# Moving K and V of the fourth attention into earlier stages, waiting for weights a stage later, and a shared expert with features on partitions

## The chip, the cores and the metric

One Trainium2 chip, one of its cores. The metric is device time in microseconds (us), lower is better. TensorE is PE in the profile, VectorE DVE, ScalarE ACT, GpSimd POOL, and SyncE, which only issues transfers here, SP.

## What is computed

A residual stream x of 4 x 256 tokens with 256 features (1024 tokens in all), and a context of the same size. Eight layers, each `x = x + layer(layernorm(x))`: an attention and a feed-forward layer, four times. The parts that the change touches:

- second attention: softmax attention of q (from x) over the context and over k, v made from x. It reads the context as it is.
- third feed-forward: `relu(x W1.T)**2`, normalised by the root of its mean square, times `W2.T`, with ternary weights.
- fourth attention: 16 heads of 16 features, all 1024 queries over all 1024 keys. `q = x Wq + bq`, `k, v = ctx Wkv + bkv`; q and k are rounded to 127 steps per token and head, v per feature over all tokens; the softmax is rounded to 255 steps per row; then a projection. K and V depend on the context and on weights alone.
- fourth feed-forward: 8 routed experts (512 hidden features, each token goes to two) and one shared expert, `silu(x Wg) * (x Wu) @ Wd` with 1024 hidden features.

## The kernel before, in words

Tokens lie on partitions in 8 tiles of 128 (`X`), or features on partitions in 2 chunks of 128 (`XT`, and `CT` for the context). Each layer is a function of its own with one or two blocks; inside a block every engine runs a list of its own, tied by semaphores, and a block ends when all engines have reached its end, SP among them. So a wait of SP at the end of a block holds all the others.

`layer_norm` (L156) runs ahead of each layer: it normalises x, turns it into `XT`, and meanwhile SP loads the weights of a later stage (L179) and waits for them (L181) before the block can end. It has two options: `ahead` projects the context's tokens on PE before the turning of x (L151, 16 matmuls of 256 columns), `ahead_features` the context's features (L721, 8 matmuls of 512 columns). A float32 matmul shows as two records. Before the change the third attention uses the second option, the fourth attention the first.

`attention_l1` (L1523) is the second attention; its first block projects q, k and v of x (L1556 and on), 8 groups of 2 matmuls with 512 columns, then v.

`ffn_relu2` (L1908) is the third feed-forward layer: 16 units; per unit PE makes two matmuls (L1941), ACT applies relu (L2003), DVE squares (L2018), ACT squares again for the mean, POOL adds it up (L1989). PE's down matmuls (L1946) for the first half lie between units 10 to 13, and those for the second half end the block.

The fourth attention is three functions. `quantise_l3` (L2038): PE projects q and then v (L151, L2074), DVE adds biases, finds the largest of each head, divides and rounds (L2121 to L2144), ACT scales v (L2100 to L2109), PE turns v, SP issues 22 loads of the experts' weights (L2064). `split_store` (L308) splits k into three bfloat16 parts whose sum is k (L334 to L353), turns them and q on PE (L373) and stores both to DRAM (L381). `attention_l3` (L2148) clears the ring buffers, loads 4 heads of q and k, keeps PE busy with 12 matmuls (L2237), and then runs 128 units, 16 heads of 8 query tiles: scores on PE (L2247), maximum on DVE (L2277), exponential to 8 bits on ACT (L2268), a transpose by DMA for every two units (L2209, issued by SP), a cast on POOL (L2224) and the sum over V on PE (L2257). SP also loads the head that comes three later (L2197 q, L2199 k), and an expert's weights in the middle of heads 0 and 1 (L2217). The buffers for the exponentials hold 4 pairs of units.

`moe_silu` (L1327) is the last stage. PE computes the router's logits; DVE chooses experts, PE counts (L1262 to L1268) and DVE places tokens (L1302 to L1323); POOL scatters the rows of x into DRAM, sorted by expert, in 16 indirect transfers (L1367); SP loads them back in 23 blocks (L1385). The order of PE's work is written out by hand. 39 units: 8 of the shared expert (its first 512 hidden features, one token tile each), 23 blocks, 8 of the shared expert (second half). Step n issues:

```
go_up(n); [counts at n == 1]; turn_hidden(n - 1); turn_x of block unit n + 1; go_down(n - 2)
```

`go_up` is 4 matmuls of 512 columns (L1422), `turn_hidden` 4 transposes (L1430), `turn_x` 2 (L1400), `go_down` 4 matmuls of 256 columns (L1444). All downs use one PSUM bank (7), so each waits until DVE has taken the one before (L1514 or L1516). At the end POOL gathers the experts' rows (L1375) and DVE merges them tile by tile (L1496).

## Time and profile before

| | us |
|---|---|
| median of 3 runs (lowest, highest) | 1148.74 (1146.13, 1152.38) |
| the profiled execution, its own time | 1146.27 |
| its span in the profile | 1144.3 |
| mean granted clock of TensorE in it | 0.851 of full speed |

Busy in the profile's span: PE 931.5 us (81%), DVE 620.5 (54%), ACT 539.3 (47%), POOL 254.8 (22%). The page lists the chain of work that ended last as PE for the last 20% of the span, with the lines of `moe_silu`. Busy shares are means over very different stages, and PE counts as busy when it runs at half its clock. So the stages are read one by one, by the times at which their first and last instructions stand in the timeline.

### The profile page before, as it was taken

The page shows a single profiled execution, that of the slowest core. Times are in us where ns is not written, and L with a number is a line of the kernel's source. Part 1 is how long each engine was busy: PE and PEld are TensorE (multiplying, and loading weights), DVE is VectorE, ACT ScalarE, POOL GpSimd, SP SyncE. Part 2 cuts the span into 40 slices and gives each one's busy share as a digit, 9 for nine tenths or more (in the row PEclk, how much of TensorE's full clock was granted, in tenths as well). Part 3 has the DMA queues.
Part 4 walks back from the last instruction along what each step waited for, and adds up shares of the span by engine and source line. Part 5 has one row for each costly group of instructions (what it writes and reads, how often), then busy time and mean ns, then how long its engine had stood idle before and what let it go on. Part 6 is the DMA issues. An engine that isn't in the chain of part 4 may idle for free. (4 is left out here: it accounts for less than half of the span.)

```text
span 1144.3 us, 15734 instructions
## 1 busy us (share of the span) xinstructions
PE 931.5 (81%) x5518; PEld 555.4 (49%) x5544; DVE 620.5 (54%) x1284; ACT 539.3 (47%) x807; POOL 254.8 (22%) x299
## 2 busy tenths in 40 slices
PE   5698887997895458899699547787776699999998
PEld 3244436665584144444367332343344556666665
DVE  4577745545145976354413938999996441111124
ACT  3166673222125745688431247998986122222211
POOL 4011000000000003144231104767675031000023
PEclk9599998998998689999899856555655799999999
DMA  3613301001480005765100936665653311111012
GB/s 124 146 34 77 84 12 42 0 1 51 103 63 28 0 17 177 185 139 81 47 1 1 349 129 120 129 108 112 107 100 70 111 46 60 43 46 46 28 46 84
DMA packets 116494, 90.07 MB, mean 79 GB/s; under 512 B 77829, under 2 KB 104655, under 8 KB 114639
## 3 DMA queue, kind: packets, MB, share of 16 engines
q1 hardware_dynamic: 111570, 81.87, 30.6%
q0 software_dynamic: 1536, 4.20, 1.2%
q10 hardware_dynamic: 3312, 3.02, 0.8%
q8 instruction: 45, 0.74, 0.3%
q14 instruction: 31, 0.25, 0.1%
HBM read 57.66 MB, written 16.38 MB: 65 GB/s over the span
## 5 line engine op out<-in xcount | busy, mean ns | idle before, releaser
L2268 ACT ACTIVATE sb_l_E<-PS,sb_l_NB,sb_L3SQS 128x1024 uint8<-128x1024 f32 x128 | 154.5, 1207 | 23.0 <-DVE sb_l_NB L2280 13.5
L2277 DVE TENSOR_REDUCE sb_l_NM<-PS 128x1 f32<-128x1024 f32 x128 | 155.4, 1214 | 3.8 <-PE PS L2247 3.8
L2247 PE MATMUL PS<-sb_l_K,sb_l_Q 128*128 128x512 bf16 x232 | 115.7, 590 | 43.0 <-ACT sb_l_E L2268 33.9
L2224 POOL CAST sb_l_ET<-sb_l_EP 128x1024 bf16<-128x1024 uint8 x128 | 129.4, 1043 | 64.1 <-DMA sb_l_EP<-sb_l_E 59.6
L682 DVE TENSOR_REDUCE sb_negmax<-PS 128x2 f32<-128x512 f32 x128 | 84.1, 689 | 32.2 <-PE PS L532 31.9
L1468 ACT ACTIVATE sb_hidden<-PS 128x512 f32<-128x512 f32 x39 | 23.3, 598 | 164.5 <-PE PS L1422 164.5
L1503 DVE TENSOR_TENSOR sb_hidden<-sb_hidden,PS 128x512 f32<-128x512 f32 x39 | 26.8, 687 | 125.1 <-ACT sb_hidden L1468 125.1
L2257 PEld LDWEIGHTS PS<-sb_L3VI,sb_l_ET 128*128 128x128 bf16 x1024 | 56.1, 113 | 69.1 <-issue 56.1
L668 ACT ACTIVATE sb_E<-PS 128x1024 f32<-128x1024 f32 x64 | 65.5, 1024 | 42.8 <-PE PS L595 42.8
L1422 PE MATMUL PS<-sb_L3w,sb_block_xT 128*128 x184 | 82.8, 592 | 0.0
L991 ACT ACTIVATE sb_E<-PS 128x1024 f32<-128x1024 f32 x64 | 65.3, 1024 | 24.7 <-PE PS L899 21.0
L532 PE MATMUL PS<-sb_K,sb_Q 96*128 96x256 bf16 x256 | 53.8, 302 | 15.8 <-ACT sb_negmax_T L642 10.3
L915 POOL MEMSET sb_rms_eps<- 128x1 f32 x1 | 0.1, 99 | 275.2 <-POOLq L175 275.2
L1422 PE MATMUL PS<-sb_W,sb_XT 128*128 128x512 f32 x128 | 59.1, 607 | 0.0
L2257 PE MATMUL PS<-sb_L3VI,sb_l_ET 128*128 128x16 bf16 x1024 | 50.8, 179 | 5.7 <-POOL sb_l_ET L2224 5.7
L1193 DVE SCALAR_TENSOR_TENSOR sb_X<-PS,sb_gates,sb_X 128x256 f32<-128x256 f32 x80 | 33.2, 476 | 35.7 <-PE PS L1116 35.7
L1422 PEld LDWEIGHTS PS<-sb_L3w,sb_block_xT 128*128 128x128 f32 x184 | 34.8, 190 | 34.4 <-issue 33.2
L200 PE MATMUL PS<-sb_identf,sb_XN 128*128 128x128 f32 x128 | 24.7, 374 | 32.3 <-DVE sb_XN L235 32.3
L532 PEld LDWEIGHTS PS<-sb_K,sb_Q 96*128 96x128 bf16 x256 | 21.3, 102 | 51.3 <-ACT sb_negmax_T L642 16.5
L595 PE MATMUL PS<-sb_Q,sb_K 128*128 128x512 bf16 x128 | 39.6, 391 | 5.3 <-DMA sb_Q<-sb_negmax_T 5.3
L1444 PE MATMUL PS<-sb_W2E,sb_hidden_T 128*128 x184 | 43.5, 379 | 0.0
L1375 POOL DMA_INDIRECT sb_XN<-ys,sb_slot x8 | 7.6, 952 | 160.0 <-PE PS L1444 157.8
(342 smaller groups left out, 1748.3 us busy)
## 6 DMA issues: line engine op xcount, KB each, us to landing
sb_Q<-q SPq DMA_DIRECT2D x48, 192.0 KB
sb_L3w<-L3w SPq DMA_DIRECT2D x16, 512.0 KB, 9.5
sb_K<-k SPq DMA_DIRECT2D x24, 192.0 KB
sb_W2E<-L3w SPq DMA_DIRECT2D x8, 512.0 KB, 9.4
q<-sb_q_parts SPq DMA_DIRECT2D x12, 256.0 KB, 2.4
xs<-zero_row SPq DMA_DIRECT2D x1, 2944.0 KB, 47.9
sb_block_x<-xs SPq DMA_DIRECT2D x23, 128.0 KB, 2.2
ys<-sb_block_y ACTq DMA_DIRECT2D x23, 128.0 KB, 2.4
```

Of the source, the lines that this page charges most:

```text
L532: ins = pe.matmul(core.PS[:, shared_bank(("max", m)), i * SEQ:(i + 1) * SEQ], Q[0:RK, g % RING, j * TOK + t * P:j * TOK + (t + 1) * P], K[ ...
L595: ins = pe.matmul(core.bank(2 * (s % 2) + n).rearrange("p (j q) -> p j q", q=SEQ), K[0:ROWS, g % RING, keys], q[:, 2 * n:2 * n + 2, b * SE ...
L668: act.activation(E[:, s % ERING].rearrange("p j q -> p (j q)"), core.PS[:, 2 * (s % 2):2 * (s % 2) + 2, :].rearrange("p b n -> p (b n)"), ...
L682: dve.tensor_reduce(NM[:, g, 2 * b:2 * b + 2, j:j + 1], core.bank(shared_bank(("max", m))).rearrange("p (u k) -> p u k", k=SEQ), axis=AX.X ...
L991: act.activation(E[:, s % ERING].rearrange("p j q -> p (j q)"), core.PS[:, 2 * (s % 2):2 * (s % 2) + 2, :].rearrange("p b n -> p (b n)"), ...
L1422: ins = pe.matmul(core.bank(2 * (u % 2) + side), x, w, start=(c == 0), stop=(c == NC - 1))
L1444: ins = pe.matmul(core.PS[:, 7, 0:D], HT[:, u % 2, k, :], w, start=(k == 0), stop=(k == HC - 1))
L2224: return eng.tensor_copy(ET[:, u % CRING], EP[:, u // 2 % TRING, :, :, u % 2])
L2247: ins = pe.matmul(core.bank(2 * (n % SRING) + half), Q[:, h % RING, t * P:(t + 1) * P], K[:, h % RING, half * HALF:(half + 1) * HALF], sta ...
L2257: ins = pe.matmul(core.PS[:, 6 + h % 2, t * HD:(t + 1) * HD], ET[:, u % CRING, k, :], VI[:, k, h * HD:(h + 1) * HD], start=(k == 0), stop= ...
L2268: act.activation(E[:, n // 2 % ERING, :, n % 2], S(n), ACT.Exp, bias=NB[:, n:n + 1], scale=scale_of(h, t), accum_out=ZS[:, n:n + 1]).then_ ...
L2277: dve.tensor_reduce(NM[:, n:n + 1], S(n), axis=AX.X, op=ALU.max, negate=True).then_inc(maxed, 1)
```

## The change

- **Weights.** `layer_norm` no longer waits for the loads that it issues; the next normalisation waits for them before it issues its own (`at_once` keeps the old wait in the first). PE waits there too, when it projects ahead.
- **V of the fourth attention.** Its weights are loaded during the first attention (4 more loads). The third normalisation projects V ahead (`ahead_features`), the first block of the second attention rounds it on ACT and DVE, and two transposes by DMA bring it into place; the clearing of `xs` comes behind them on SP.
- **K.** The normalisation ahead of `ffn_relu2` projects K (`ahead`), the one behind it no longer does. `ffn_relu2` rounds K and splits it on DVE and ACT between its own steps (`key_step`), three DMA transposes of 128 x 2048 turn the parts, and 6 stores bring them to DRAM. The first 10 experts' loads are issued at the start of this function, 6 at its end, in front of its last waits.
- **The fourth attention.** `quantise_l3` and `split_store` are gone. `attention_l3` projects q itself, rounds it in two halves on DVE, turns it on PE in bfloat16 and copies it to SBUF; each head's q is then copied three times from there (3 transfers where there was 1). Two experts' loads go ahead of q's, ten more transfers follow in the middle of heads 0 to 9: 6 of experts and the 4 of the last stage (router, gate, up, down weights) that the last normalisation issued before.
- **The last stage.** A unit of the shared expert is now one chunk of 128 hidden features for 512 tokens: weights are stationary and `XT` moves, so the hidden values come out with features on partitions and need no turning. It has 8 units for the first 512 tokens and 8 for the others. The downs (8 matmuls of 256 columns for each of the 8 token tiles) need all 8 chunks: tiles 0 to 3 are done in steps 9 to 12, between the first blocks, tiles 4 to 7 all after the last unit. The order inside a step is up, turn, shared down, `turn_x`, block down.

```diff
+                if sent_by_now:
+                    sp.wait_ge(core.weights_in, sent_by_now)
                 for dst, src in weights:
-                    sp.dma_start(dst, src).then_inc(loaded, 16)
-                if weights:
-                    sp.wait_ge(loaded, 16 * len(weights))
+                    sp.dma_start(dst, src).then_inc(core.weights_in, 16)
+                if at_once:
+                    sp.wait_ge(core.weights_in, core.weights_sent)
...
+                if sent_by_now and (ahead is not None or ahead_features is not None):
+                    pe.wait_ge(core.weights_in, sent_by_now)
...
-    units = ([("shared", 0, t) for t in range(NT)] + [("block", None, b) for b in range(BLOCKS)]
-             + [("shared", 1, t) for t in range(NT)])
+    SC = 2 * HC
+    units = ([("shared", 0, k) for k in range(SC)] + [("block", None, b) for b in range(BLOCKS)]
+             + [("shared", 1, k) for k in range(SC)])
     NU = len(units)
-    block_unit = lambda b: NT + b
+    block_unit = lambda b: SC + b
+    downs_at = [[] for n in range(NU + 2)]
+    for b in range(BLOCKS):
+        downs_at[block_unit(b) + 2].append(("block", b))
+    for t in range(4):
+        downs_at[SC + 1 + t].insert(0, ("shared", t))
+        downs_at[NU + 1].append(("shared", 4 + t))
+    downs = [d for at in downs_at for d in at]
+    down_count = {d: i + 1 for i, d in enumerate(downs)}
...
-                            x = core.XT[:, c, i * P:(i + 1) * P]
-                            w = WGU[:, side, c, half * HID:(half + 1) * HID]
+                            x = WGU[:, side, c, i * P:(i + 1) * P]
+                            w = core.XT[:, c, half * HALF:(half + 1) * HALF]
...
+            def go_down(kind, i):
+                if down_count[(kind, i)] >= 2:
+                    pe.wait_ge(y_out, down_count[(kind, i)] - 1)
+                if kind == "shared":
+                    pe.wait_ge(hidden, SC if i < 4 else NU)
+                    for k in range(SC):
+                        ins = pe.matmul(core.PS[:, 7, 0:D], HS[:, k, (i % 4) * P:(i % 4 + 1) * P], WD[:, k, :],
+                                        start=(k == 0), stop=(k == SC - 1))
+                else:
+                    pe.wait_ge(h_out, i + 1)
+                    for k in range(HC):
                         w = core.W2E[:, bass.ds(expert[i], 1), k * D:(k + 1) * D].rearrange("p e n -> p (e n)")
-                    ins = pe.matmul(core.PS[:, 7, 0:D], HT[:, u % 2, k, :], w, start=(k == 0), stop=(k == HC - 1))
+                        ins = pe.matmul(core.PS[:, 7, 0:D], HT[:, i % 2, k, :], w, start=(k == 0), stop=(k == HC - 1))
                 ins.then_inc(down, 1)
...
-                if 1 <= n <= NU:
-                    turn_hidden(n - 1)
+                if 1 <= n <= NU and units[n - 1][0] == "block":
+                    turn_hidden(units[n - 1][2])
+                for d in downs_at[n]:
+                    if d[0] == "shared":
+                        go_down(*d)
...
+                        if i >= 4:
                             merge(i)
-
-
-def attention_l1(core, dram, Wq, Wk, Wv, Wo, xs):
+                if n == NU - SC + 7:
+                    for t in range(4):
+                        merge(t)
...
+                for c in range(NC):
+                    sp.wait_ge(v3_rounded, c + 1)
+                    sp.dma_start_transpose(VI[:, :, c * P:(c + 1) * P], VQ[:, c, :]).then_inc(v3_turned, 16)
+                sp.wait_ge(v3_turned, 16 * NC)
...
+            @block.sync
+            def _(sp):
+                for dst, src in experts[:SOON]:
+                    sp.dma_start(dst, src).then_inc(core.experts_in, 16)
+                def turn(i):
+                    sp.wait_ge((k_high, k_middle, k_low)[i], NT // 2)
+                    if i >= 2:
+                        sp.wait_ge(k_stored[i - 2], 16 * NC)
+                    sp.dma_start_transpose(KT[i % 2], KP[:, i].rearrange("p t d -> p (t d)")).then_inc(k_turned[i], 16)
+
+                def store(i):
+                    sp.wait_ge(k_turned[i], 16)
+                    for c in range(NC):
+                        sp.dma_start(k16[8 * c:8 * c + 8, 16 * i:16 * i + 16, :],
+                                     KT[i % 2].rearrange("p (t c) n -> p t c n", c=NC)[:, :, c, :]).then_inc(k_stored[i], 16)
+
+                turn(0)
+                turn(1)
+                store(0)
+                store(1)
+                turn(2)
+                store(2)
+                for dst, src in experts[SOON:]:
+                    sp.dma_start(dst, src).then_inc(core.experts_in, 16)
+                for i in range(PARTS):
+                    sp.wait_ge(k_stored[i], 16 * NC)
...
+                    if 11 <= n <= 14:
+                        b = n - 11
+                        act.wait_ge(k_back, b + 1)
+                        act.activation(pair(KP[:, 0], b), pair(KB, b), ACT.Copy).then_inc(k_high, 1)
+                    if 13 <= n <= 16:
+                        b = n - 13
+                        act.wait_ge(k_rest, b + 1)
+                        act.activation(pair(KP[:, 1], b), pair(KR, b), ACT.Copy).then_inc(k_middle, 1)
...
+                def key_step(n):
+
+                    if n < 4:
+                        dve.tensor_tensor(pair(KB, n), core.bank(4 + n).rearrange("p (t d) -> p t d", d=D),
+                                          bk.unsqueeze(1).to_broadcast([P, 2, D]), ALU.add).then_inc(k_copied, 1)
+                    elif n < 8:
+                        b = n - 4
+                        dve.wait_ge(k_copied, b + 1)
+                        dve.tensor_reduce(SK[:, 2 * b:2 * b + 2, :].rearrange("p t h -> p (t h)"), heads(KB, b), axis=AX.X,
+                                          op=ALU.max, apply_absolute_value=True).then_inc(k_maxed, 1)
+                    elif n == 8:
+                        dve.wait_ge(k_maxed, NT // 2)
+                        dve.tensor_scalar(SK[:, :, :], SK[:, :, :], 1.0 / 127.0, 1e-8, ALU.mult, ALU.max).then_inc(k_scaled, 1)
+                    elif n == 9:
+                        dve.wait_ge(k_scaled, 1)
+                        dve.reciprocal(IV[:, :, :], SK[:, :, :]).then_inc(k_inverse, 1)
+                    elif n <= 13:
+                        b = n - 10
+                        dve.wait_ge(k_inverse, 1)
+                        dve.tensor_tensor(heads(KB, b), heads(KB, b), of_heads(IV, b), ALU.mult).then_inc(k_ratio, 1)
+                        dve.wait_ge(k_ratio, b + 1)
+                        dve.tensor_scalar(pair(KB, b), pair(KB, b), MAGIC, -MAGIC, ALU.add, ALU.add).then_inc(k_whole, 1)
+                        dve.wait_ge(k_whole, b + 1)
+                        dve.tensor_tensor(heads(KB, b), heads(KB, b), of_heads(SK, b), ALU.mult).then_inc(k_back, 1)
+                    if 12 <= n <= 15:
+                        b = n - 12
+                        dve.wait_ge(k_high, b + 1)
+                        dve.tensor_tensor(pair(KR, b), pair(KB, b), pair(KP[:, 0], b), ALU.subtract).then_inc(k_rest, 1)
+                    if 14 <= n <= 17:
+                        b = n - 14
+                        dve.wait_ge(k_middle, b + 1)
+                        dve.tensor_tensor(pair(KP[:, 2], b), pair(KR, b), pair(KP[:, 1], b), ALU.subtract).then_inc(k_low, 1)
+
                 for n, (th, k) in enumerate(units):
                     dve.wait_ge(relued, n + 1)
                     dve.tensor_tensor(H[:, th, k, :], R[:, n % 2, :], R[:, n % 2, :], ALU.mult).then_inc(squared, 1)
+                    key_step(n)
+                key_step(16)
+                key_step(17)
...
+                def load_k(h):
+                    sp.dma_start(K[0:ROWS, h % RING, :], ks[h]).then_inc(q_in[h % RING], 16)
+
+                def load_q(h):
+                    for i in range(PARTS):
+                        sp.dma_start(Q[HD * i:HD * (i + 1), h % RING, :], QT[HD * (h % 8):HD * (h % 8 + 1), h // 8, :]
+                                     ).then_inc(q_in[h % RING], 16)
+
                 def load(h):
-                    if h >= RING:
-                        sp.wait_ge(scored, NT * (h - RING + 1))
-                    sp.dma_start(Q[0:ROWS, h % RING, :], qs[h].unsqueeze(1).to_broadcast([HD, PARTS, TOK])
-                                 ).then_inc(q_in[h % RING], 16)
-                    sp.dma_start(K[0:ROWS, h % RING, :], ks[h].rearrange("(i d) t -> d i t", i=PARTS)
-                                 ).then_inc(q_in[h % RING], 16)
+                    sp.wait_ge(scored, NT * (h - RING + 1))
+                    load_k(h)
+                    load_q(h)
 
                 sp.wait_ge(cleared, 2)
                 for h in range(RING):
-                    load(h)
+                    load_k(h)
+                for dst, src in experts[:QUICK]:
+                    sp.dma_start(dst, src).then_inc(core.experts_in, 16)
+                sp.wait_ge(out_a, 2)
+                for h in range(RING):
+                    load_q(h)
+                sp.wait_ge(out_v, 2)
...
+                for half in range(2):
+                    project_tokens(pe, core, core.XT, Wq, D, 0, range(4 * half, 4 * half + 4)).then_inc(projected, 1)
+                for half in range(2):
+                    pe.wait_ge(q_whole, half + 1)
+                    for c in range(NC):
+                        for j in range(4):
+                            ins = pe.transpose(core.bank_bf16(4 + 2 * half + c)[:, j * P:(j + 1) * P],
+                                               QI[:, 4 * half + j, c * P:(c + 1) * P], core.identb[:, :])
+                        ins.then_inc(q_turned, 1)
+                pe.wait_ge(out_a, 2)
+                pe.wait_ge(out_v, 2)
...
+                for half in range(2):
+                    act.wait_ge(q_turned, 2 * half + 1)
+                    act.activation(QT[:, 0, half * HALF:(half + 1) * HALF], core.bank_bf16(4 + 2 * half)[:, 0:HALF],
+                                   ACT.Copy).then_inc(out_a, 1)
+                act.preload_act_table_set("exp_and_others")
...
+                for half in range(2):
+                    dve.wait_ge(projected, half + 1)
+                    dve.tensor_tensor(half_of(QF, half), core.PS[:, 2 * half:2 * half + 2, :].rearrange(
+                        "p b (u d) -> p (b u) d", d=D), bq.unsqueeze(1).to_broadcast([P, 4, D]), ALU.add).then_inc(q_copied, 1)
...
+                    dve.tensor_tensor(heads(QF, half), heads(QF, half), of_heads(IQ, half).unsqueeze(2).to_broadcast(
+                        [P, 4 * HEADS, HD]), ALU.mult).then_inc(q_ratio, 1)
+                    dve.wait_ge(q_ratio, half + 1)
+                    dve.tensor_scalar(half_of(QI, half), half_of(QF, half), MAGIC, -MAGIC, ALU.add, ALU.add
+                                      ).then_inc(q_whole, 1)
+                for half in range(2):
+                    dve.wait_ge(q_turned, 2 * half + 2)
+                    dve.tensor_copy(QT[:, 1, half * HALF:(half + 1) * HALF], core.bank_bf16(5 + 2 * half)[:, 0:HALF]
+                                    ).then_inc(out_v, 1)
...
-        attention_l1(core, dram, w["L1wqT"], w["L1wkT"], w["L1wvT"], w["L1woT"], scratch["xs"])
+        VI = core.sb(ctx, "L3VI", [P, NT, D], BF16)
+        SV = core.sb(ctx, "L3SV", [P, NC], F32)
+        layer_norm(core, loads, ahead_features=Wv3)
+        attention_l1(core, dram, w["L1wqT"], w["L1wkT"], w["L1wvT"], w["L1woT"], scratch["xs"], bv3, VI[:, :, :],
+                     SV[:, :])
...
+        w_next["L3Wp"] = Wv3
+        loads.append((Wv3, dram["L3Wp"].rearrange("(c p) n -> p c n", p=P)))
+        layer_norm(core, loads, ahead=Wk3)
...
+        ffn_relu2(core, w["L2W1"], w["L2W2"], bk3, scratch["k16"], first_half, core.W[0][:, 3 * D:3 * D + 3 * TOK])
...
-            with ExitStack() as c5:
-                QI = core.sb(c5, "L3QI", [P, NT, D], BF16)
-                KF = core.sb(c5, "L3KF", [P, NT, D], F32)
-                bvt = w["L3bvT"].rearrange("p c n -> p (c n)")
-                quantise_l3(core, w["L3Wq"], w["L3Wv"], w["L3bq"][:, 0, :], w["L3bk"][:, 0, :], bvt,
-                            QI[:, :, :], KF[:, :, :], VI[:, :, :], SQS[:, :], SV[:, :], first_half + second_half[2:])
-                split_store(core, [
-                    (QI[:, :, :], D, 1, lambda i, c: scratch["q16"][8 * c:8 * c + 8]),
-                    (KF[:, :, :], D, PARTS, lambda i, c: scratch["k16"][8 * c:8 * c + 8, 16 * i:16 * i + 16, :])])
-            attention_l3(core, scratch["q16"], scratch["k16"], VI, SQS, second_half[0:2],
-                         16 * len(first_half + second_half))
+            attention_l3(core, w["L3Wq"], w["L3bq"][:, 0, :], scratch["k16"], VI, SQS[:, :], second_half + shared,
+                         16 * len(first_half + second_half + shared), core.W[0][:, 3 * D:3 * D + TOK])
...
-        layer_norm(core, [(router[:, :, :], dram["L3router"].rearrange("(c p) n -> p c n", p=P)),
-                          (WGU[:, 0], dram["L3wg"].rearrange("(c p) n -> p c n", p=P)),
-                          (WGU[:, 1], dram["L3wu"].rearrange("(c p) n -> p c n", p=P)),
-                          (WD[:, :, :], dram["L3wd"].rearrange("(c p) n -> p c n", p=P))])
+        layer_norm(core, [])
```

## Rows read from the trace of the kernel before

**Rows 1.** Windows: length, PE, PEld, DVE, ACT, POOL busy, clock, DMA share, GB/s
```profile
280.60:289.30 8.70, 3.56 (x16) 3.10 (x16) 4.02 (x18) 3.74 (x8) 0.00 (x0) 0.70 0.72 242
...
356.20:362.10 5.90, 3.31 (x16) 2.89 (x16) 4.02 (x18) 3.76 (x9) 0.00 (x0) 0.71 0.42 133
...
426.00:435.10 9.10, 8.85 (x32) 4.62 (x32) 4.02 (x18) 3.86 (x8) 0.00 (x0) 1.00 0.69 230
...
550.70:558.60 7.90, 3.34 (x16) 2.92 (x16) 4.02 (x18) 3.75 (x8) 0.00 (x0) 0.72 0.55 168
...
558.60:619.80 61.20, 58.75 (x208) 38.85 (x209) 17.61 (x36) 18.27 (x34) 19.06 (x17) 0.97 0.00 0
...
619.80:631.40 11.60, 10.58 (x48) 8.99 (x49) 4.03 (x18) 3.86 (x8) 0.02 (x1) 0.85 0.01 1
...
684.10:883.00 198.90, 147.94 (x1274) 75.79 (x1300) 181.08 (x291) 168.50 (x259) 131.23 (x129) 0.56 0.58 107
...
895.00:906.80 11.80, 3.56 (x16) 3.12 (x17) 4.03 (x18) 3.78 (x9) 0.03 (x1) 0.71 0.77 267
```

**Rows 2.** Timeline, start of the third feed-forward layer
```profile
558.64 7.88 PE L1941 MATMUL PS<-sb_XT,sb_W2E 128*128 128x512 f32 x14 [3.04 <-PEq L175]
...
563.99 0.60 ACT L2003 ACTIVATE sb_relu<-PS 128x512 f32<-128x512 f32 x1 [1.12 <-PE PS L1941]
```

**Rows 3.** Timeline, the fourth attention's preparation up to its first scores
```profile
631.42 2.29 DVE L2121 TENSOR_TENSOR sb_l_kf<-PS,sb_W 128x2048 f32<-128x2048 f32 x1 [0.30 <-PEq L175]
...
643.59 0.95 DVE L2132 RECIPROCAL sb_l_iq<-sb_L3SQS 128x128 f32<-128x128 f32 x1
...
684.53 4.37 PE L2237 MATMUL PS<-sb_L3VI,sb_identb 128*128 128x512 bf16 x11 [10.94 <-PEq L330]
...
689.51 0.82 PE L2247 MATMUL PS<-sb_l_K,sb_l_Q 128*128 128x512 bf16 x3 [0.61 <-DMA sb_l_K<-k]
```

**Rows 4.** Landing of line 838's transposes (128x2048), then line 381's stores, timeline
```profile
DMA to landing us min/median/max: 4.2/8.0/11.7
...
672.67 6.31 SPq L381 DMA_DIRECT2D k<-sb_tb  x6
```

**Rows 5.** Timeline, DVE and POOL in the third attention
```profile
443.19 0.68 DVE L1025 TENSOR_TENSOR sb_rest<-sb_rms_normed,sb_k_parts 128x512 f32<-128x512 f32 x1
...
444.63 1.16 POOL L921 TENSOR_TENSOR sb_k_parts<-sb_rest,sb_k_parts 128x512 bf16<-128x512 f32 x1 [5.38 <-DVE sb_k_parts L1031]
...
445.06 1.27 DVE L1025 TENSOR_TENSOR sb_rest<-sb_rms_normed,sb_k_parts 128x512 f32<-128x512 f32 x1
```

**Rows 6.** Landing of line 2209's transposes; an expert's load; the stretch behind it
```profile
DMA to landing us min/median/max: 3.0/3.1/4.9
...
712.20 1.81 SPq L2217 DMA_DIRECT2D sb_W2E<-L3w  x1
...
712.50:724.00 11.50, 9.47 (x80) 4.73 (x80) 11.19 (x19) 10.39 (x17) 7.99 (x9) 0.50 0.84 155
```

**Rows 7.** Timeline, the first routed block of the last stage
```profile
952.00 3.69 SPq L1385 DMA_DIRECT2D sb_block_x<-xs  x5
...
954.96 0.38 PE L1400 MATMUL PS<-sb_identf,sb_block_x 128*128 128x128 f32 x2
...
956.90 1.51 PE L1422 MATMUL PS<-sb_L3w,sb_block_xT 128*128 x3
```

**Rows 8.** Chain that ended last: start, length, what; the last stage
```profile
1107.52 3.43 PE PS L1422 x8
...
1111.39 1.73 PE PS L1444 x8
...
1133.35 0.44 PE PS L1430 x4
...
1138.12 0.43 DVE sb_X L1516
...
1138.69 1.98 PE PS L1444 x8
```

359 lines of the change are left out of this document (132 added, 227 removed).

## The prediction

> **What bounds the kernel now.** The stages follow one another, so I read them one at a time: first the windows by stage, then the timeline at each border, then the chain that ended last, for the last stage. In the windows, the normalisations differ though they do the same work: 5.9 us where few weights are loaded, 7.9, 8.7 and 11.8 us where more are, at a DMA share up to 0.77 [rows 1]. DVE's work in all of them is 4.0 us, so what is above 5.9 is the wait for weights (or PE, in the two of 9.1 and 11.6 us that project something ahead). The third feed-forward layer is PE's (58.8 of 61.2 us busy at 0.97 of the clock); the fourth attention's 128 units are DVE's (11.19 of 11.5 us in a head's stretch), with PE at a granted clock of 0.50, the lower of its two levels (1.2 of 2.4 GHz), in most of it [rows 1, 6]. Between 631.4 and 689.5 us the fourth attention only prepares: 58.1 us of DVE, ACT and stores one after another [rows 3]. In the last stage the chain is PE alone until the final downs: per shared unit 3.43 us of up, 0.44 of turning and 1.73 of down [rows 8].
>
> **The parts, each against its stage before.**
>
> 1. *Third normalisation, V.* PE now has 8 matmuls of 512 columns there, as the one of 9.1 us has, but it starts idle. What a cold start costs: in the third feed-forward layer relu of unit 1 starts 5.35 us after the first matmul [rows 2], while a unit takes 3.43 / 2 = 1.72 us at full clock (4 matmuls of that width are 3.43 us [rows 8]), so 5.35 - 2 x 1.72 = 1.9, nearly all of it in the first unit. So 9.1 + 1.8 - 8.7 = +2.2; the attention behind it then starts warm, -1.8. Sum +0.4. V's rounding (ACT 6 passes, DVE one maximum of 2.3 us as the 2048-wide operation of [rows 3]) and two DMA transposes lie beside 20 us of projections; queued behind them on SP is only the clearing of xs, for which the last stage waits some 600 us later. With the cover gone it would be 10 us. The 4 extra loads in the first attention go between others: 0.
>
> 2. *Normalisation before the third feed-forward layer, K.* It becomes what the next one was: 11.6 - 7.9 = +3.7; the layer starts warm: -1.8. Sum +1.9. The next one becomes a plain one, 5.9 - 11.6 = -5.7.
>
> 3. *K in the third feed-forward layer.* DVE's square and a key step are below 1.4 us of a unit's 1.72, so units 0 to 9 keep PE's pace; units 10 to 13 have 5.2 us each. The steps from unit 13 on do not fit: some 12 operations of 0.35 to 0.7 us remain, and POOL's adds lie between them. What POOL does to DVE: the same subtraction takes 0.68 us alone and 1.27 when POOL's runs from 0.43 us before it, that is, it ends 0.54 us after POOL's end [rows 5]. I get the low parts of K ready 9 to 11 us before the block's old end, PE's own path unharmed because the squares are needed late. Behind it on SP: the last transpose also waits for the first stores; it lands 4.2 us or more after its issue; before, 6 stores took from 672.7 us to the block's end at 684.1, 1.9 us each [rows 4, 3]; so two more stores and their landing are 5. After them SP issues 6 experts' loads, 3 us, and only then waits. First stores done 4 us before the old end at best, transpose +5, issues and stores +5: the block ends 6 us late. The end nearest above nothing is 0 (all of it covered by PE's last 17 us), the far one 12 (transposes at their median of 8.0, stores at twice their time). I take +6.
>
>    The DVE-POOL effect is also a rule of the Trainium skill (SBUF — State Buffer, "SBUF: two separate sides"): a DVE operation with two SBUF inputs or in a fast mode and a GpSimd operation exclude each other for a whole instruction. By that rule, the trace agrees. Without it the low parts would be ready 3 us earlier and the term would be +3.
>
> 4. *The fourth attention's preparation.* Before, 58.1 us. Now, from the block's start: PE projects the first half of q, 8 matmuls of 256 columns, 3.43 + 1.8 for the cold start = 5.3 us. DVE per half: three operations at half of 2.29, a rounding of 0.6, the reciprocal at half of 0.95 and two small ones with handovers, 0.6: 5.2 us, so the halves end at 10.5 and 15.7. Turning 0.8, ACT's and DVE's copies until 17.4; then SP's three copies of head 0 (1.8 us of issues, 2.3 to land) until 21.4, beside PE's 12 warming matmuls of 4.4 [rows 3], which end at 21.9 and so are what ends last. First scores at 22.3: -35.8. Ends: 19 if the warming overlaps, 26 if experts' transfers delay q's.
>
> 5. *The 128 units.* Bound by DVE, unchanged. SP gets 4 issues of 0.6 per head instead of 2, and an expert's or shared weight's load in 10 heads instead of 2. In head 1, where such a load held SP for 1.81 us, DVE stayed at 11.19 of 11.5 [rows 6]. A buffer pair comes round after 4 pairs, 11.5 us; three of them, 8.6 us, stand against a landing of 3.1 plus up to 4.2 of other issues. I take +0.5; ends 0 and 6.
>
> 6. *Last normalisation.* Its 3 MB are loaded earlier: 5.9 - 11.8 = -5.9.
>
> 7. *The last stage.* The change removes 16 turnings, 16 x 0.44 = 7.0 us of PE. But it also takes the downs out of the first 8 units, and those units cover the routing. Their rows reach SP at 952.00 and the first block can go up about 955.3 (before: 956.90, and PE turned the block at 954.96 without a wait of its own) [rows 7]. Of what PE did before its up at 956.90, 6 downs and 7 turnings no longer come first: 956.9 - 10.4 - 3.1 = 943.4, and about 1 us more since DVE's placing of the tokens now holds one up, so PE is through at 944.5. It stands for 10 us and then starts cold. Counted: block 0 starts 1.6 us earlier, but what it has behind it is less: before, one turning and two downs of the first half were left (3.9 us), now four downs of twice the length (13.8): +9.9 - 1.6; cold start +1.8; three block downs that follow a shared one wait for DVE on bank 7, 0.45 each: +1.4. Second half until its last up: 5 downs and 7 turnings fewer, -11.7. After the last up: before 1133.35 to 1140.67, 7.3 us; now 1.4 for silu and product, then four downs of 3.7 (twice 1.73 and the 0.25 that the isolated down of 1.98 shows), with DVE's add and handovers of 0.6 between [rows 8], and 0.4 for the four merges put ahead: 18.4, +11.1. Sum +10.9, I take +10.5. Nothing else is late: gathers start about 14 us before the last up's end and need 20; their first merge is the 38th step's.
>
> **Sum.** 0.4 + 1.9 - 5.7 + 6 - 35.8 + 0.5 - 5.9 + 10.5 = -28.1 us. The profiled execution took 1146.3 us, 2.5 below the median: it would take 1118; for the median of runs, 1148.7 - 28.1 = 1120.6, and I forecast 1120.
>
> **Rivals.**
>
> - *K covered.* The landings are short with an idle DMA, and the block ends at its old time: 1114. For it, the stretch's DMA share of 0.00 in [rows 1]; against, four transfers in a row that wait for one another. Chance 0.18.
> - *K later still.* 1126 to 1130, if stores go at half their rate. The trace has no store of this form. Here the source is in pieces of 256 bytes: the Trainium skill (DMA: Bandwidth & Descriptors, "Specifications") names 512 bytes as the least for full rate; no row shows its price on a store. By twice the 1.9 us per store [rows 4], four stores on the path add 7.6: 1128. Chance 0.14.
> - *The last stage gains what it removes.* If PE did not stand (rows ready earlier than I count), -7.0 + 3 instead of +10.5: 1106. Against it stands the 952.00 of [rows 7], which the change does not move. Chance 0.07.
> - *V holds its block.* If the transposes of V come only after the projections, the second attention is 5 us later: 1125. This is the part that could fail to do what it says. Chance 0.05.
> - *Slower: SP's queue in the fourth attention.* Each head's 4 issues (2.4 us) and a load (1.8) stand ahead of a transpose; ACT then waits for a free pair and DVE behind it. It decides from 5.5 us of delay. If all of it came through, 12 heads x 2.4 + 10 loads x 1.8 = 47 us: 1167. Against it: head 1. Chance 0.05.
> - The forecast as it stands: 0.51.
>
> A measurement can tell this kernel from no change above about 0.5%, 5.7 us. The first four rivals and the forecast are faster by far more; half-paid SP delay gives 0.02 for the same. So faster 0.93, same 0.02, slower 0.05. The range 1107 to 1132 takes in both K cases, V, and 4 us more on the last stage either way, and leaves out SP's case and most of the third.
>
> **What would show it.** Right: first scores 22 us after the last preparation's block starts; PE idle for about 10 us before the first routed block and half the clock behind it; last downs 4.3 us apart; last normalisation 5.9 us; the third feed-forward stage 67 us by SP's waits. Wrong: DVE below 11.1 us in a head's stretch, PE busy through the routing, or a normalisation before the second attention above 11.5 us.

## The result and the profile after

The changed kernel takes 1131.55 us (median of 4 runs, 1129.71 to 1132.27) against 1150.56 us for the kernel before on the same chip (1146.13 to 1155.61): a ratio of 0.9843, 95% interval 0.9816 to 0.987. That is 19 us, 1.6%, where 28 were forecast; the median lies half a microsecond inside the upper end of the forecast range, 1132. The profiled execution took 1129.71 us with a span of 1128.0, so between the two profiled executions, the forecast's own base, the change is worth 16.3 us of span.

I read it in the order of the prediction, stage by stage. The windows of the changed kernel (length, PE, PEld, DVE, ACT, POOL busy, clock, DMA share, GB/s) are: third normalisation with V; the one with K; the third feed-forward layer until its last statistics; what follows until the next normalisation; that normalisation; the fourth attention's preparation; its units; the last normalisation; then two stretches around the first routed blocks.

```profile
282.10:293.70 11.60, 11.29 (x32) 5.61 (x33) 4.02 (x18) 3.88 (x9) 0.00 (x0) 0.79 0.54 182
551.10:563.80 12.70, 11.66 (x49) 9.80 (x49) 4.02 (x18) 3.86 (x8) 0.06 (x1) 0.78 0.19 53
563.80:623.10 59.30, 57.10 (x208) 38.13 (x208) 43.22 (x66) 22.61 (x42) 20.01 (x17) 1.00 0.39 121
623.10:635.70 12.60, 0.00 (x0) 0.00 (x0) 0.00 (x0) 0.00 (x0) 0.00 (x0) 0.57 0.69 153
635.70:641.90 6.20, 3.69 (x16) 3.09 (x16) 4.03 (x18) 3.75 (x8) 0.00 (x1) 0.50 0.99 403
641.90:664.30 22.40, 14.68 (x62) 10.25 (x64) 11.09 (x16) 2.48 (x3) 3.54 (x2) 0.77 0.26 74
664.30:856.20 191.90, 141.09 (x1254) 70.97 (x1276) 179.30 (x290) 165.84 (x257) 128.69 (x128) 0.57 0.69 135
869.50:875.50 6.00, 3.49 (x17) 3.09 (x17) 4.01 (x18) 3.79 (x9) 0.04 (x1) 0.72 0.00 0
911.80:921.00 9.20, 0.01 (x1) 0.00 (x0) 0.69 (x1) 0.60 (x1) 4.64 (x5) 0.68 0.31 107
921.00:970.50 49.50, 43.83 (x157) 28.26 (x158) 5.97 (x11) 7.13 (x15) 0.00 (x0) 0.92 0.10 28
```

The fourth row is the find. In 12.6 us no engine has a computing instruction; only the DMA works. The third feed-forward layer itself ended where it should (59.3 us against 61.2 before [rows 1]); the block did not. SP's timeline over that end (start, length, line, what; the length is the time in which SP issues, not the transfer):

```profile
607.73 1.72 SPq L1945 DMA_TRANSPOSE sb_W<-sb_l_k_parts  x1
612.42 1.92 SPq L1945 DMA_TRANSPOSE sb_l_k_turned<-sb_l_k_parts  x1
614.38 2.81 SPq L1950 DMA_DIRECT2D k<-sb_W  x2
617.24 4.34 SPq L1950 DMA_DIRECT2D k<-sb_l_k_turned  x2
621.69 4.53 SPq L1945 DMA_TRANSPOSE sb_W<-sb_l_k_parts  x1
627.97 2.25 SPq L1950 DMA_DIRECT2D k<-sb_W  x2
630.27 4.86 SPq L1960 DMA_DIRECT2D sb_L3w<-L3w  x6
```

VectorE confirms where the stand begins and ends: its last statistics end at 623.0, and then

```profile
635.71 0.38 DVE L237 BATCH_NORM_AGGREGATE sb_ln_mv<-sb_ln_st 128x2 f32<-128x6 f32 x4 [12.70 <-PEq L1936]
```

The fourth attention's preparation answers to [rows 3]. From the block's start to the first scores it took 58.1 us, now 21.8 (PE's timeline):

```profile
641.93 8.87 PE L155 MATMUL PS<-sb_W,sb_XT 128*128 128x256 f32 x32 [1.03 <-PEq L180]
652.83 0.62 PE L2229 MATMUL PS<-sb_identb,sb_W 128*128 128x128 bf16 x8 [2.02 <-DVE sb_W L2293]
658.12 1.03 PE L2229 MATMUL PS<-sb_identb,sb_W 128*128 128x128 bf16 x8 [4.67 <-DVE sb_W L2293]
660.15 3.70 PE L2235 MATMUL PS<-sb_L3VI,sb_identb 128*128 128x512 bf16 x11 [0.99 <-DVE sb_l_qt L2297]
663.69 1.46 PE L2245 MATMUL PS<-sb_l_K,sb_l_Q 128*128 128x512 bf16 x6
```

The first routed blocks of the last stage answer to [rows 7]. PE stands for 9.3 us until the first rows arrive, the first block's up then takes 6.4 us instead of 3.7, and two more waits of 1.6 and 1.3 us follow, where before none was:

```profile
921.08 0.69 PE L1346 MATMUL PS<-sb_identf,sb_block_x 128*128 128x128 f32 x2 [9.27 <-DMA sb_block_x<-xs]
923.31 6.38 PE L1368 MATMUL PS<-sb_L3w,sb_block_xT 128*128 x8 [1.54 <-issue]
929.52 0.38 PE L1346 MATMUL PS<-sb_identf,sb_block_x 128*128 128x128 f32 x2
931.50 3.70 PE L1368 MATMUL PS<-sb_L3w,sb_block_xT 128*128 x8 [1.59 <-DVE sb_hidden L1458]
935.03 0.60 PE L1376 MATMUL PS<-sb_identf,sb_hidden 128*128 128x128 f32 x4
935.47 3.62 PE L1386 MATMUL PS<-sb_L3wd,sb_shared_hidden_T 128*128 128x256 f32 x16
938.92 0.38 PE L1346 MATMUL PS<-sb_identf,sb_block_x 128*128 128x128 f32 x2
940.62 3.69 PE L1368 MATMUL PS<-sb_L3w,sb_block_xT 128*128 x8 [1.32 <-ACT sb_block_xT L1429]
```

And the end, which answers to [rows 8]:

```profile
1085.72 20.76 PE L1368 MATMUL PS<-sb_XT,sb_W 128*128 128x512 f32 x48
1107.99 3.69 PE L1386 MATMUL PS<-sb_L3wd,sb_shared_hidden_T 128*128 128x256 f32 x16 [1.50 <-DVE sb_shared_hidden_T L1458]
1112.19 3.72 PE L1386 MATMUL PS<-sb_L3wd,sb_shared_hidden_T 128*128 128x256 f32 x16 [0.51 <-DVE sb_X L1469]
1116.42 3.72 PE L1386 MATMUL PS<-sb_L3wd,sb_shared_hidden_T 128*128 128x256 f32 x16 [0.51 <-DVE sb_X L1469]
1120.66 3.72 PE L1386 MATMUL PS<-sb_L3wd,sb_shared_hidden_T 128*128 128x256 f32 x16 [0.51 <-DVE sb_X L1469]
```

Three lengths serve as rulers from here on. The **feed-forward stretch** runs from the first aggregation of the normalisation ahead of the third feed-forward layer to the first of the next: 69.05 us before, 84.60 after. The **last stage** runs from the router's first matmul to VectorE's last operation: 235.3 before, 250.4 after. It has three pieces, before and after: to the first routed block's up 50.1 and 47.8; from there to the last block's up 128.1 and 146.05; from there to the end 57.2 and 56.5. The two stages hold the whole miss. The stages ahead vary from profile to profile, whatever the edit: the first attention from 179 to 188 us, the first feed-forward layer from 91.8 to 94.5, the third attention from 124.0 to 126.6. That is why stage lengths decide here where two totals differ by a few us. They have a spread of their own. Where the edit does not touch it, the last stage is 250.4 to 250.6 us in all seven profiles; the feed-forward stretch is 83.1 to 84.7 us in seven profiles, and the 84.60 of the changed kernel is near its upper end.

### The profile page after: what moved, and what is told of

The parts are those of the page before. It is cut to its first block and busy times, and to the rows that moved or that the text cites. A ratio compares the mean times of both kernels' runs of the same rounds, so it can differ in the third digit from the quotient of the medians.

```text
span 1128.0 us, 15444 instructions
## 1 busy us (share of the span) xinstructions
PE 923.5 (82%) x5390; PEld 540.5 (48%) x5416; DVE 622.5 (55%) x1304; ACT 527.2 (47%) x794; POOL 253.1 (22%) x297
## 5 line engine op out<-in xcount | busy, mean ns | idle before, releaser
L2271 ACT ACTIVATE sb_l_E<-PS,sb_l_NB,sb_L3SQS 128x1024 uint8<-128x1024 f32 x128 | 154.5, 1207 | 21.9 <-DVE sb_l_NB L2305 12.4
L1368 PE MATMUL PS<-sb_L3w,sb_block_xT 128*128 x184 | 85.7, 610 | 4.5 <-DVE sb_hidden L1458 1.6
L1458 DVE TENSOR_TENSOR sb_hidden<-sb_hidden,PS 128x512 f32<-128x512 f32 x23 | 15.8, 687 | 100.1 <-ACT sb_hidden L1423 100.1
L1423 ACT ACTIVATE sb_hidden<-PS 128x512 f32<-128x512 f32 x23 | 13.7, 598 | 104.0 <-PE PS L1368 104.0
L1368 PE MATMUL PS<-sb_XT,sb_W 128*128 128x512 f32 x128 | 58.1, 611 | 0.9 <-DVE sb_shared_hidden_T L1458 0.9
L1125 DVE SCALAR_TENSOR_TENSOR sb_X<-PS,sb_gates,sb_X 128x256 f32<-128x256 f32 x80 | 33.2, 477 | 35.8 <-PE PS L1048 35.8
```

The lines of the kernel that those rows point to most:

```text
L1368: ins = pe.matmul(core.bank(2 * (u % 2) + side), x, w, start=(c == 0), stop=(c == NC - 1))
L2271: act.activation(E[:, n // 2 % ERING, :, n % 2], S(n), ACT.Exp, bias=NB[:, n:n + 1], scale=scale_of(h, t), accum_out=ZS[:, n:n + 1]).then_ ...
```

## The experiments

All are made from the changed kernel, the later ones on top of earlier edits where it is said. Where no interval is given, it is a single run. Expectations count the last stage to the end of the span, some 2 us behind VectorE's last operation.

### The last stage in its old form

```diff
-    SC = 2 * HC
-    units = ([("shared", 0, k) for k in range(SC)] + [("block", None, b) for b in range(BLOCKS)]
-             + [("shared", 1, k) for k in range(SC)])
+    units = ([("shared", 0, t) for t in range(NT)] + [("block", None, b) for b in range(BLOCKS)]
+             + [("shared", 1, t) for t in range(NT)])
...
```

The rest of `moe_silu` goes back to its old form with it.

> The changed kernel with the last stage in its form of before (shared expert with tokens on partitions, 16 turnings). Between router start and the end the changed kernel took 252.5 us, the one before 237.5. Theory (the new form of the shared expert itself costs the 15.0 us, whatever stands ahead of it): the last stage falls back to 237.5 +- 1 us, the whole kernel to 1131.5 - 15 = 1116.5. Rival (a good part of the 15.0 comes from elsewhere, the weights in other places or rows that arrive later): the last stage stays above 242 us and the kernel above 1121.

Measured: 1112.65 us, ratio 0.9687 (0.9657 to 0.9716). The last stage is 233.8 us: 16.6 less than after, and even 1.5 less than before, because the router's matmuls now follow PE's last work by 1 us instead of 6.7 and take 5.1 us instead of 7.0 (granted clock in them 0.70 instead of 0.50). It ends below the 237.5 +- 1 us expected, so the theory holds and is even too mild: the new form of the shared expert costs 16.6 us like for like. It is the change's most expensive part.

### K's end: four experiments

```diff
-    HEADS, HD, SOON = 16, 16, 10
+    HEADS, HD, SOON = 16, 16, 16
```

> The changed kernel with all 16 experts' loads of the third feed-forward block issued at its start; none behind K's stores. There the six issues occupied SP for 4.9 us after the last store's issue. Theory A (the end is set by SP's queue of issues): the stretch from the start of the normalisation before this block to the one behind it, 84.6 us, becomes 79.7. Theory B (the last store's landing sets the end and the six issues lay beside it): 84.6 stays, or falls by 1 us at most. The landing was not visible; before, stores landed about 4 us after issue, so 80.5 is between the two.

Measured: the stretch is 83.5 us, 1.1 shorter, which is within the spread of the profiles without this edit. Theory B: the six issues lay beside the landing of the last stores and stood out by less than 1 us, if at all (the chain ahead of them was 0.3 us quicker too). With nothing behind the stores the windows show the landing itself:

```profile
626.50:628.80 2.30, 0.00 (x0) 0.00 (x0) 0.00 (x0) 0.00 (x0) 0.00 (x0) 0.50 0.21 42
628.80:632.50 3.70, 0.00 (x0) 0.00 (x0) 0.00 (x0) 0.00 (x0) 0.00 (x0) 0.50 0.53 116
632.50:633.30 0.80, 0.00 (x0) 0.00 (x0) 0.00 (x0) 0.00 (x0) 0.00 (x0) 0.50 0.00 0
```

SP has issued the last store at 628.76, the data moves until 632.5 at 116 GB/s, and the next block starts at 633.38: 4.6 us from the last issue's end to the next block's first operation. The Trainium skill (Perfetto Trace Analysis, "DMA Instruction — HWDGE (DVE, Sync)") says that such a row covers the wait for the descriptor unit, its use and the push of the semaphore, and that the time in which the data moves is not in it. By that rule, the trace agrees, the last two stores are 2.3 us of issue with 3.7 us of movement behind it.

```diff
-        KP = core.sb(ctx, "l3_k_parts", [P, PARTS, NT, D], BF16)
+        KP = core.sb(ctx, "l3_k_parts", [P, PARTS, NC, NT, P], BF16)
...
-                                     KT[i % 2].rearrange("p (t c) n -> p t c n", c=NC)[:, :, c, :]).then_inc(k_stored[i], 16)
+                                     KT[i % 2].rearrange("p (c t) n -> p c t n", c=NC)[:, c]).then_inc(k_stored[i], 16)
...
```

> The changed kernel with K's parts laid out so that each store reads pieces of 2048 contiguous bytes of a partition instead of 256 (its 8 token blocks one behind the other). The six stores' issues took 0.6 to 2.2 us each on SP. Theory A (the small pieces make stores slow, in the issue and in the transfer): issues fall to about 0.6 us each, the stretch of the third feed-forward layer from 84.6 to 76 to 79 us. Theory B (transposes and waiting on one another make the length): issues and stretch stay within 1.5 us of 84.6.

Measured: 81.3 us, 3.3 shorter, between the two. The issues did fall to 0.6 to 0.8 us each (mean of a pair):

```profile
614.39 1.90 SPq L1947 DMA_TRANSPOSE sb_l_k_turned<-sb_l_k_parts  x1
616.33 1.59 SPq L1952 DMA_DIRECT2D k<-sb_W  x2
618.90 1.28 SPq L1952 DMA_DIRECT2D k<-sb_l_k_turned  x2
622.36 3.65 SPq L1947 DMA_TRANSPOSE sb_W<-sb_l_k_parts  x1
627.50 1.18 SPq L1952 DMA_DIRECT2D k<-sb_W  x2
```

The pieces of 256 bytes are thus worth 3.3 us of the stretch against this profile of the changed kernel, 1.8 against the shortest of the seven, mostly in the queue; but now SP waits for the transposes to land, and the last two stores still can't be issued before 627.5, 13.1 us after the second transpose's issue.

```diff
-                        pool.tensor_tensor(SUM[:, th, :], SUM[:, th, :], S4[:, n % 2, :], ALU.add).then_inc(pooled, 1)
+                        pool.tensor_tensor(SUM[:, th, 0:8], SUM[:, th, 0:8], S4[:, n % 2, 0:8], ALU.add).then_inc(pooled, 1)
```

> The changed kernel with GpSimd's 14 adds of the sums of squares cut from 512 to 8 columns (so the sums of squares are left out but for 8 tokens in 512). Question: do these adds, which lie across VectorE's steps for K (single operations of 1.7 to 3.0 us instead of 0.7), set the block's end? Theory A (SP's queue of transposes, stores and issues sets the end): VectorE's operations come down to 0.7, the low parts of K are ready 2 to 4 us earlier, the first transpose 1 to 2 us earlier, and the stretch falls by that 1 to 2 us only: 82.6 to 83.6. Rival (readiness of the low parts sets the end): it falls by 3 us or more, below 81.6.

Measured: 81.2 us, 3.4 shorter (1.8 against the shortest of the seven), so it falls on the rival's side, and neither theory had the place right. VectorE's long operations are gone (the last three steps for the low part take 1.9 us together, where they took 2.96). One multiplication in the changed kernel with GpSimd's add beside it, and the same with the short adds:

```profile
603.14 1.77 DVE L2074 TENSOR_TENSOR sb_XN<-sb_XN,sb_W 128x512 f32<-128x512 f32 x1
603.10 1.26 POOL L2020 TENSOR_TENSOR sb_h_sq_sum<-sb_h_sq_sum,sb_h_sq 128x512 f32<-128x512 f32 x1 [3.90 <-ACT sb_h_sq L2041]
...
606.90 0.70 DVE L2074 TENSOR_TENSOR sb_XN<-sb_XN,sb_W 128x512 f32<-128x512 f32 x1
```

Counted from the stretch's start, the first transpose is issued at 54.3 us (56.6 after) and the second at 58.0 (61.3 after), and from the second on every row of SP stands 3.2 to 3.4 us earlier. What starts the chain is the readiness of the middle part, not of the low one: behind it SP is never free before 621.7. So VectorE's contention with POOL sets the start of the chain, and SP's queue its length.

```diff
-                turn(2)
-                store(2)
-                for dst, src in experts[SOON:]:
-                    sp.dma_start(dst, src).then_inc(core.experts_in, 16)
-                for i in range(PARTS):
-                    sp.wait_ge(k_stored[i], 16 * NC)
...
+    def later(sp):
+        sp_of.append(sp)
+        turn(2)
+        store(2)
+    return later, experts[SOON:]
...
+                for stored in k_stored:
+                    sp.wait_ge(stored, 16 * NC)
...
```

SP of the next normalisation calls `later`; the waits of the last added lines stand in `attention_l3`, in front of the loads of K.

> The changed kernel; the third feed-forward block ends without waiting for K's stores. Its last transpose and two stores are issued in the normalisation behind it, the stores are waited for in the fourth attention, and the six experts' loads go there too, behind the loads of K. Theory (the 12.7 us in which VectorE stands at the block's end are SP's queue and its landings, and nothing else needs them): the stretch of the third feed-forward layer falls from 84.6 to about 72, the normalisation gains at most 2 us, the 22 us of preparation stay: 1131.5 - 11 = 1120.5 us. Rival (the transfers only move, and the preparation or the first heads wait for K or for q behind six loads): 1127 us or more.

Measured: 1120.05 us, ratio 0.976 (0.972 to 0.9799). The stretch falls by 12.75 us to 71.85; the normalisation behind lasts 1.3 us longer, until SP has issued; the preparation takes 22.0 us to its first scores. The theory holds: in the changed kernel all of the stand is transfers that nothing behind the block needs for 10 us more.

### The first half's shared downs

```diff
     for t in range(4):
-        downs_at[SC + 1 + t].insert(0, ("shared", t))
+        downs_at[(SC - 1, SC - 1, SC, SC + 1)[t]].append(("shared", t))
...
```

The loops that issue the downs of a step change with it: ahead of the first block's unit all of them come before `turn_x`, from it on behind.

> The changed kernel with the first half's four shared downs placed otherwise: two before the first routed block's rows are turned, one behind each of the next two blocks' turning (where PE waited 1.6 and 1.3 us for the copy of the turned rows). The work is the same. From the first routed block's up to the last one's, the changed kernel takes 146.05 us, the one before 128.06. Theory (the 18.0 us are downs that come too late to lie under the routing, the lower clock after the stand, and waits that a down used to cover): 131 us, and the whole 1131.5 - 15.8 = 1115.7. Rival (the double-length downs cost this wherever they lie): 140 us or more, the whole above 1125.

Measured: 1116.24 us, ratio 0.9722 (0.9685 to 0.9758). The piece is 131.1 us, as worked out, and the last stage 235.3. The same downs now fill the stand:

```profile
911.45 3.72 PE L1386 MATMUL PS<-sb_L3wd,sb_shared_hidden_T 128*128 128x256 f32 x16 [1.41 <-DVE sb_shared_hidden_T L1458]
915.69 3.72 PE L1386 MATMUL PS<-sb_L3wd,sb_shared_hidden_T 128*128 128x256 f32 x16 [0.51 <-DVE sb_X L1469]
919.45 0.44 PE L1346 MATMUL PS<-sb_identf,sb_block_x 128*128 128x128 f32 x2
921.42 3.70 PE L1368 MATMUL PS<-sb_L3w,sb_block_xT 128*128 x8 [1.53 <-issue]
924.96 0.38 PE L1346 MATMUL PS<-sb_identf,sb_block_x 128*128 128x128 f32 x2
925.17 3.62 PE L1386 MATMUL PS<-sb_L3wd,sb_shared_hidden_T 128*128 128x256 f32 x16
928.63 3.60 PE L1368 MATMUL PS<-sb_L3w,sb_block_xT 128*128 x8
```

The first block's up takes 3.70 us again, and the down at 925.17 lies where PE waited 1.6 us.

```diff
+                if n == SC - 1:
+                    for i in range(18):
+                        pe.matmul(core.bank(7), core.identf[:, :], HS[:, 0, :], start=True, stop=True)
```

> The changed kernel with 18 matmuls of 512 columns and no use put in PE's idle time of 9.3 us ahead of the first routed block. Question: what is the stand itself (rows not there), and what the lower clock behind it? Theory: the first block's eight matmuls take 3.6 instead of 6.4 us, the stretch from its start to the last block's falls from 146.05 to about 143; the first up starts as late as before. Rival (the clock plays no part, the 6.4 us have another cause): 6.4 stays.

Measured: 1139.81 us in one run, longer than the changed kernel, and the last part of the expectation missed: I took such a matmul for 0.43 us, it takes 0.86 (four of them are the 3.43 us of an up), so the 18 ran for 15.4 us and the first up started 5.7 us late. What it was made for it tells all the same: that up takes 3.69 us (granted clock 1.00, where the up of 6.38 us had 0.58) and the piece behind is 143.4 us, 2.65 shorter. So the lower clock behind the stand costs 2.7 of the 18 us; the two waits behind the turned rows stay at 1.62 and 1.32 us at full clock, and are another 2.9. Only a part of them is ACT's copy of those rows: in the changed kernel the copies end at 930.60 and 939.72 us, and each up starts 0.9 us later. In the code the read of the block's expert number (`value_load`) stands in that place of PE's list; no run here separates it.

This edit is made on top of the one of the two early downs:

```diff
+            def go_down_late(k):
...
+                for t in range(4):
+                    ins = pe.matmul(core.PS[:, 4 + t, 0:D], HS[:, k, t * P:(t + 1) * P], WD[:, k, :],
+                                    start=(k == 0), stop=(k == SC - 1))
...
+                if n >= U1 + 2:
...
+                    go_down_late(n - U1 - 2)
```

> On top of the two-early form: the second half's four shared downs are accumulated in four banks of PSUM, eight parts each, every part two units behind the hidden unit it reads, and the merges of the routed results come before the last unit's product. Theory (the tail's 19.6 us from the last up's end to VectorE's last operation hold 3 us of handovers on one bank and of standing): from the last routed block's up to the end 55.3 us instead of 58.6, the whole 1112.4. Rival (matmuls switching banks and weights every 256 columns run slower than a down in one piece, or the merges delay the products): 58 us or more.

Measured: 1116.76 us. To the end of the span, as the expectation counts, the last piece is 53.7 us, 4.9 less than the 58.6 after, where 3.3 were expected: the merge behind the last add, 1.0 us, went too, and I had not counted it. The last stage is 230.1 us, against 235.3 with the two early downs alone. The total is no lower than with these and 4.4 us above its expectation, because earlier stages of this execution, untouched by the edit, were longer: the last normalisation starts at 876.8 us, against 869.5 in the changed kernel and 867.8 in the profiled run with the two early downs. The parts in four banks take 0.43 us each, two rows of 0.22, the pace of a down in one piece:

```profile
1101.77 1.89 PE L1405 MATMUL PS<-sb_L3wd,sb_shared_hidden_T 128*128 128x256 f32 x8
1103.50 3.60 PE L1372 MATMUL PS<-sb_XT,sb_W 128*128 128x512 f32 x8
1106.93 5.34 PE L1405 MATMUL PS<-sb_L3wd,sb_shared_hidden_T 128*128 128x256 f32 x24
```

### Together

The edit of the first run is the sum of the three (K's end, the early downs, the downs by part). The second has the old last stage and K's end.

> The changed kernel with the three edits tried singly: K's last transfers finished in the blocks behind, the first half's shared downs before and in the first routed blocks, the second half's accumulated by part. They lie in different stages, so they should add: 1131.5 - 11.1 - 15.1 - 5.1 = 1100 us, ratio to before 0.957. Rival (they interact: the rows' transfers or the clock change when the stages ahead are shorter): above 1105.

Measured over 5 rounds: 1098.97 us (1098.34 to 1103.36), ratio to before 0.9573 (0.9546 to 0.9601). The three edits add up: feed-forward stretch 71.6, last stage 230.2. It is the fastest version of this study, 33 us below the changed kernel and 50 below the one before.

> The changed kernel with the last stage in its form of before and K's last transfers finished in the blocks behind. By the stages: 1112.65 - 11.1 = 1101.5 us, ratio 0.959. Beside the version with the mended shared expert it tells whether features on partitions is worth anything when its downs lie well: by stages the mended form is 233.8 - 230.1 = 3.7 us shorter from the router to VectorE's last operation.

Measured over 5 rounds: 1106.86 us (1101.25 to 1107.8), ratio 0.9619 (0.9592 to 0.9647). Its last stage is 233.8 us as in the first experiment, its feed-forward stretch 71.8; the total is 5 us above the expectation, and in its profiled run the first attention takes 184.8 us, where the profiled run of the first experiment had 179.2; for the other runs no profile tells. So the new form of the shared expert is worth 3.6 us by the last stage (230.2 against 233.8) where all its downs lie well. With the early downs alone it was 235.3, still 1.5 more than the old form: the gain comes with the downs by part, and no run gives the old form such a tail. The totals' intervals touch (0.9592 to 0.9601), so the size rests on the stage.

### The two smaller parts

```diff
-def layer_norm(core, weights, ahead=None, ahead_features=None, at_once=False):
+def layer_norm(core, weights, ahead=None, ahead_features=None, at_once=True):
```

> The changed kernel in which every normalisation waits for its own loads again, as before; the places of the loads stay as changed. Theory (the wait moved to the next normalisation is worth little by itself: where loads are long, V or K projected ahead covers them, and what shortened the last two normalisations is that they load nothing): no stretch grows by more than 2 us, the whole 1131 to 1135. Rival (the later wait is what pays): the second, fourth and fifth normalisation grow by 2 us or more each, the whole above 1137.

Measured: 1134.36 us. No stretch between the second normalisation's start and the last one's end differs by more than 2 us from the changed kernel's (94.0, 74.8, 70.1, 124.8, 83.5, 234.1 us against 92.1, 74.9, 70.2, 124.0, 84.6, 233.8). The one of 1.9 us, behind the second, also reads 94.3 us in other runs with the later wait. Most of the rest between the two profiles is in the first attention (184.9 against 182.0). Waiting in the next normalisation is worth too little to be seen here; the last normalisation keeps its 6.0 us in this run too, so its 5.7 us come from the place of its 3 MB of loads, the fourth attention.

```diff
-    ROWS, WARM = 48, 12
+    ROWS, WARM = 48, 0
```

> The changed kernel without the 12 matmuls that keep PE busy while the fourth attention waits for q's first transfers. In the prediction they were what ends last there, 0.5 us behind q. Theory: the first scores start at most 1 us earlier after the block's start (21.8 us there), and the whole stays within 1 us of the changed kernel's stage length of 233.8. Rival (the warming work is what the first scores wait for): 3 us earlier or more.

Measured: 1131.82 us; the first scores start 21.5 us after the block's start instead of 21.8, and PE's wait names what it is for:

```profile
664.98 2.34 PE L2245 MATMUL PS<-sb_l_K,sb_l_Q 128*128 128x512 bf16 x5 [4.03 <-DMA sb_l_Q<-sb_l_qt]
```

Without the warming work the first scores start 0.5 us behind the landing of the first head's q (664.47 us), with it 1.0 us behind (662.68 and 663.69). So it held them by half a microsecond, and q landed 0.2 us later in this run, which leaves the 0.3. Taking it out gives nothing: the first scores take longer instead (five matmuls 2.34 us, where six took 1.46), and the stage is 234.1 us.

## Where the prediction was right and wrong

Its direction held, and most of its terms; the range held by half a microsecond only, since the number was 11.5 us too low against the median. By its own steps, in us, profile against profile:

| step | predicted | measured |
|---|---|---|
| 1 third normalisation with V, and the attention behind | +0.4 | -0.8 |
| 2 normalisation with K, warm layer behind | +1.9 | +3.2 |
| 2 the next one, plain | -5.7 | -5.4 |
| 3 K at the feed-forward block's end | +6 | +12.4 |
| 4 the fourth attention's preparation | -35.8 | -36.3 |
| 5 its 128 units | +0.5 | +0.2 |
| 6 last normalisation | -5.9 | -5.7 |
| 7 last stage | +10.5 | +15.0 |
| stages not in the sum | 0 | +1.1 |
| sum | -28.1 | -16.3 |

*Step 3 failed*, by 6.4 us: K at the feed-forward block's end, taken for 6, cost 12.4 (the stand of 12.7 us less the 0.3 of any border between blocks). The mechanism was the one named (SP's serial chain of transposes, stores and issues outlasts PE), its sizes were not, and the far end of 12 was nearer than the 6 I took. By the sum's three terms: the first stores were to be done 4 us before the block's old end, at 618 in this trace (551.1 + 69.05 + 1.9 = 622.1); they were done at 621.6, 3.5 us late. The transpose was to take 5 and took 6.3. Issues, stores and landing were to take 5, and from the transpose's landing to the next block's first operation it was 7.7. That is 7.6 us in all, of which 1.3 stand in step 2.

The prediction had the low part ready 9 to 11 us before the block's old end; it was ready 7.5 us before it (614.6). That did not even matter, since SP was busy with the first four stores until 621.6. The stores of the old preparation, 1.05 us of issue each and 1.9 with their landing [rows 4, 3], were the wrong measure for a form in pieces of 256 bytes, whose first four took 1.4 and 2.2 us of issue. Of the old transposes' landings (4.2, 8.0 in the median, 11.7 at most [rows 4]) I put nearly the least into the sum and the median only into the far end; the three here took 4.2, 4.3 and 6.3.

Small pieces stood there as a rival, "K later still", with 0.14. The experiment with 2048-byte pieces gives them 3.3 us, 1.8 at least. The Trainium skill (DMA: Bandwidth & Descriptors, "Specifications") gives 512 bytes as the smallest transfer for line rate; the experiment agrees in its direction, but it does not separate the rate of the data from the number of pieces. GpSimd's adds beside VectorE, which were in the prediction, set the start of the chain and are worth as much by experiment (3.4 us, 1.8 at least). How the two share the miss stays open: no run has both edits.

The six issues, 3 us in the prediction, took 4.9. Its sum left no room for them of their own, since its 5 us were already what two stores and their landing had been given, and that was right: they lay beside the landing (1.1 us by experiment, no more than the spread).

*Step 7 failed*, by 4.5 us, in one of its four items. Until the first block's up I had -1.6, it is -2.3; from the last block's up to the last up's end -11.7, it is -11.2; the tail +11.1, it is +10.6. Between the first and the last block's up I had +13.1 (the downs, the cold start, three waits on bank 7), it is +18.0. The cold start was 2.7, not 1.8. The three steps with a wait on bank 7 gave 2.0, not 1.4 (9.9 to 10.0 us against 5.8 of a plain step, for a down of 3.45). And 2.9 us were not in the sum at all: PE's waits between turned rows and up, in the two blocks that have no down to lie in front of them. About half a microsecond stays without a name. The chain before showed none of these waits, since there a down of 1.73 us covered each; taking the down away uncovers it, and the run with a down put there again has no such wait (the up at 928.63). I named the places from which the change takes work, and did not ask what that work had covered. That the routing uncovers PE for 9 to 10 us was right (9.3), and so was the handover of 4.3 us in the tail (4.2).

*Step 4 was right in its items*: the first half of q is there after 5.5 us (predicted 5.3), the halves' roundings 10.8 and 16.1 us from the block's start (10.5 and 15.7), the scores at 21.8. The prediction had the scores wait for the warming matmuls by half a microsecond behind q, and by the experiment that is what they did.

Steps 1, 2, 5 and 6 were within 1.3 us. Of step 1's -0.8, the normalisation is +2.9 and the attention behind -3.6; 2.0 of these are a wait of PE for ACT that only the profile of before shows in that attention, so I put them down to that execution and not to the change. No wait for SP's queue appeared in the fourth attention: a head's stretch still has 11.2 of 11.5 us of VectorE, and the slower rival fell with it. V did not hold its block: its transposes were issued at 304.3 us, 50 us before PE's last matmul there.

## What to carry to other kernels

When a step moves into another block, cost its serial chain on the issuing queue by transfers in pieces of the same size, and not with the fastest landing on record, and ask whether the block has to wait for it at all: here the transfers were harmless, and the wait for them at the block's end was 12.7 us. When an edit takes work out of a pipelined loop, list the waits that this work covered; the idle time it uncovers is first place for other work that has no deadline, and 15 us came back here from moving four downs by a few places. Stage lengths from two profiles settle what totals can't, where an unrelated stage varies by several us, as long as the difference is larger than the spread of the stage itself: 0.2 us for the last stage here, 1.7 for the feed-forward stretch.
